# Routed experts: a third pair of buffers for the weighed outputs, the gather moved ahead of the scatter, and loads of weights released by the first half of a scatter

## The reference, cut to what matters

```python
x = x + 0.5 * ffn(layernorm(x)); x = x + attention(layernorm(x)); x = x + 0.5 * ffn(layernorm(x))
# ffn, h = the 4096 normalised tokens, xb[e] = the up to 192 tokens of expert e
g = einsum('ech,eih->eci', xb, w_gate); u = einsum('ech,eih->eci', xb, w_up)
yb = einsum('eci,ehi->ech', silu(g) * u, w_down)        # E = 32 experts, H = 512, I = 256
routed = sum over the 6 experts of a token of yb[expert, its slot] * its weight
return routed + shared_expert(h)
```

## Time and profile before

| | |
|---|---|
| median of 3 runs | 1670.54 us (1665.2 to 1672.09) |
| the profiled execution | 1662.59 us, span 1660.8 us |
| mean granted TensorE clock | 0.962 |
| busy in the span | PE 89%, DVE 66%, ACT 62%, POOL 45% |
| moved by DMA | 257.61 MB, mean 155 GB/s |

### The profile page before, as it was taken

How to read it: one execution, slowest core, us unless ns; L and a number is a source line. 1 busy time by engine, 2 the same in 40 slices (tenths; PEclk the granted TensorE clock), 3 DMA queues, 4 the chain that set the end, 5 groups by cost and what they waited for, 6 DMA issues and landing times. The chain is left out here.

```text
span 1660.8 us, 23985 instructions
## 1 busy us (share of the span) xinstructions
PE 1476.0 (89%) x8434; PEld 1226.3 (74%) x8436; DVE 1103.8 (66%) x2094; ACT 1028.3 (62%) x2046; POOL 754.6 (45%) x655
## 2 busy tenths in 40 slices
PE   5999969989894889999999999895999869998896
PEld 4877768877773678887887887774887758877775
DVE  5659848867672466766766765664649858776774
ACT  5861448777773476666666666654762528776774
POOL 0123225655554666565556655420113224665554
PEclk9999979999997799999999999997999979999998
DMA  7736388989895101111111111006654467998895
GB/s 275 246 126 207 99 260 249 266 257 265 258 264 87 52 26 46 39 58 52 39 39 64 39 39 39 30 35 232 204 178 153 144 205 231 259 270 250 263 257 104
DMA packets 113207, 257.61 MB, mean 155 GB/s; under 512 B 21216, under 2 KB 22176, under 8 KB 112832
## 3 DMA queue, kind: packets, MB, share of 16 engines
q1 hardware_dynamic: 90560, 204.16, 37.3%
q0 software_dynamic: 22528, 51.92, 13.8%
HBM read 187.27 MB, written 68.76 MB: 154 GB/s over the span
## 5 line engine op out<-in xcount | busy, mean ns | idle before, releaser
L989 DVE TENSOR_TENSOR e_w_lo<-e_raw,e_w_hi 128x1024 fp32r<-128x1024 f32 x192 | 233.9, 1219 | 31.2 <-ACT e_w_hi L925 29.6
L925 ACT ACTIVATE e_w_hi<-e_raw 128x1024 fp32r<-128x1024 f32 x192 | 202.3, 1054 | 20.8 <-PEq L273 20.8
L1490 POOL TENSOR_SCALAR t_prob<-t_prob,t_inv 128x128 f32<-128x128 f32 (+7 forms) x128 | 111.5, 871 | 221.3 <-DVE t_inv L1395 221.3
L901 POOL DMA_INDIRECT e_xg<-htab,slots x128 | 145.7, 1138 | 58.0 <-issue 38.4
L1063 PE MATMUL e_ps_gate<-e_xt,e_w_hi 128*128 128x384 f32 x512 | 159.3, 375 | 0.0
L909 POOL DMA_INDIRECT x_after_ffn<-e_y,slots x64 | 96.4, 1506 | 121.8 <-ACT e_y L954 83.9
L1063 PE MATMUL e_ps_up<-e_xt,e_w_hi 128*128 128x384 f32 x512 | 151.0, 360 | 0.0
L909 POOL DMA_INDIRECT out<-e_y,slots x64 | 95.7, 1495 | 120.9 <-ACT e_y L954 83.6
L357 POOL TENSOR_SCALAR d_inter<-d_inter 128x512 f32<-128x512 f32 x32 | 26.2, 818 | 266.9 <-DVE d_inter L521 266.8
L1290 ACT ACTIVATE t_prob<-a_wide,t_neg_max,a_q_scale 128x128 f32<-128x128 f32 (+7 forms) x128 | 106.5, 832 | 53.8 <-DVE t_neg_max L1389 53.5
L954 ACT ACTIVATE e_y<-e_ps_down,e_xg 96x512 f32<-96x512 f32 x128 | 83.1, 679 | 90.5 <-DMA out<-e_y,slots 34.2
(11 more groups left out here) (218 smaller groups left out, 4613.5 us busy)
## 6 DMA issues: line engine op xcount, KB each, us to landing
e_raw<-in_w_experts SPq DMA_DIRECT2D x192, 512.0 KB
htab<-d_h SPq DMA_DIRECT2D x16, 1024.0 KB, 5.2
d_x<-in_x SPq DMA_DIRECT2D x16, 512.0 KB, 6.9
d_xs<-in_x SPq DMA_DIRECT2D x32, 256.0 KB, 3.5
x_after_ffn<-d_xs SPq DMA_DIRECT2D x32, 256.0 KB, 3.2
q_x<-x_after_ffn SPq DMA_DIRECT2D x32, 256.0 KB, 3.0
t_res<-x_after_ffn SPq DMA_DIRECT2D x32, 256.0 KB, 2.6
x_after_attention<-t_res SPq DMA_DIRECT2D x32, 256.0 KB, 2.0
```

The source lines that it names most:

```text
L901: pool.indirect_dma_start(xg[e % GATHERED][q][:, :], None, htab, row).then_inc(gathered[e % GATHERED], 16)
L925: act.activation(third(w_hi[e % 2], c), third(raw[e % 3], c), ACT.Copy).then_inc(hi_ready, 1)
L989: dve.tensor_tensor(third(w_lo[e % 2], c), third(raw[e % 3], c), third(w_hi[e % 2], c).bitcast(F32), ALU.subtract).then_inc(lo_ready, 1)
L1490: pool.tensor_scalar(prob[:, u, 0:width(i)], prob[:, u, 0:width(i)], inv[:, u:u + 1], 1.0, ALU.mult, ALU.mult).then_inc(p_ready, 1)
```

## The change

1. `y` gets a third pair of buffers: `weigh(e)` waits for the scatter of e - 3 instead of e - 2, half by half. `silu`, `inter`, `in_hi` and `in_lo` go down to one buffer each.
2. `added` becomes two semaphores, one for each half. A scatter still waits for both halves of the one before. The load of the weights of e + 3 waits for the first half of the scatter of e - 3 alone.
3. GpSimd waits for `y_ready` of e, issues `gather(e + 5)`, and then waits for the landing of the scatter of e - 1 and issues `scatter(e)`.

```diff
-        silu = [sb(f"e_silu{u}_", [P, TC], F32) for u in range(2)]
+        silu = sb("e_silu", [P, TC], F32)
...
-        y = [[sb(f"e_y{u}{q}_", [HALF, D], F32) for q in range(2)] for u in range(2)]
+        y = [[sb(f"e_y{r}{q}_", [HALF, D], F32) for q in range(2)] for r in range(3)]
...
-        added = sem("e_added")
+        added = [sem(f"e_added{q}_") for q in range(2)]
...
                     if e >= 3:
-                        sp.wait_ge(added, 32 * (e - 2))
+                        sp.wait_ge(added[0], 16 * (e - 2))
...
                 def scatter(e):
-                    pool.wait_ge(y_ready, 2 * e + 2)
                     if e:
-                        pool.wait_ge(added, 32 * e)
+                        for q in range(2):
+                            pool.wait_ge(added[q], 16 * e)
...
-                        pool.indirect_dma_start(acc, row, y[e % 2][q][:, :], None, compute_op=ALU.add).then_inc(added, 16)
+                        pool.indirect_dma_start(acc, row, y[e % 3][q][:, :], None, compute_op=ALU.add).then_inc(added[q], 16)
...
                 for e in range(E):
-                    scatter(e)
+                    pool.wait_ge(y_ready, 2 * e + 2)
                     if e + GATHERED < E:
                         gather(e + GATHERED)
-                pool.wait_ge(added, 32 * E)
+                    scatter(e)
+                for q in range(2):
+                    pool.wait_ge(added[q], 16 * E)
...
                 def weigh(e):
-                    if e >= 2:
-                        act.wait_ge(added, 32 * (e - 1))
                     for q in range(2):
+                        if e >= 3:
+                            act.wait_ge(added[q], 16 * (e - 2))
                         act.wait_ge(d_ready, 2 * e + q + 1)
-                        act.activation(y[e % 2][q][:, :], ps_down[q][0:HALF, :], ACT.Copy,
+                        act.activation(y[e % 3][q][:, :], ps_down[q][0:HALF, :], ACT.Copy,
```

More of the change, by code:

```diff
@@ L836, in routed_experts @@
         gate_sum, up_sum = sb("e_gate_sum", [P, FB, CAP], F32), sb("e_up_sum", [P, FB, CAP], F32)
-        silu = [sb(f"e_silu{u}_", [P, TC], F32) for u in range(2)]
-        inter = [sb(f"e_inter{u}_", [P, TC], F32) for u in range(2)]
-        in_hi = [sb(f"e_in_hi{u}_", [P, TC], F32R) for u in range(2)]
-        in_lo = [sb(f"e_in_lo{u}_", [P, TC], F32R) for u in range(2)]
-        y = [[sb(f"e_y{u}{q}_", [HALF, D], F32) for q in range(2)] for u in range(2)]
+        silu = sb("e_silu", [P, TC], F32)
+        inter = sb("e_inter", [P, TC], F32)
+        in_hi = sb("e_in_hi", [P, TC], F32R)
+        in_lo = sb("e_in_lo", [P, TC], F32R)
+        y = [[sb(f"e_y{r}{q}_", [HALF, D], F32) for q in range(2)] for r in range(3)]
         ps_t = [pb(f"e_ps_t{i}_") for i in range(2)]
@@ L941, in gate @@
                     act.wait_ge(gate_sum_ready, e + 1)
-                    act.activation(silu[e % 2][:, :], gate_sum[:, :, :].rearrange("p b s -> p (b s)"),
+                    act.activation(silu[:, :], gate_sum[:, :, :].rearrange("p b s -> p (b s)"),
                                    ACT.Silu).then_inc(silu_ready, 1)
@@ L946, in split_inner @@
                     act.wait_ge(mul_ready, e + 1)
-                    act.activation(in_hi[e % 2][:, :], inter[e % 2][:, :], ACT.Copy).then_inc(ihi_ready, 1)
+                    act.activation(in_hi[:, :], inter[:, :], ACT.Copy).then_inc(ihi_ready, 1)
                 def weigh(e):
-                    if e >= 2:
-                        act.wait_ge(added, 32 * (e - 1))
                     for q in range(2):
+                        if e >= 3:
+                            act.wait_ge(added[q], 16 * (e - 2))
                         act.wait_ge(d_ready, 2 * e + q + 1)
-                        act.activation(y[e % 2][q][:, :], ps_down[q][0:HALF, :], ACT.Copy,
+                        act.activation(y[e % 3][q][:, :], ps_down[q][0:HALF, :], ACT.Copy,
                                        scale=xg[e % GATHERED][q][:, D + e:D + e + 1]).then_inc(y_ready, 1)
@@ L1008, in gate @@
                     dve.wait_ge(silu_ready, e + 1)
-                    dve.tensor_tensor(inter[e % 2][:, :], silu[e % 2][:, :], up_sum[:, :, :].rearrange("p b s -> p (b s)"),
+                    dve.tensor_tensor(inter[:, :], silu[:, :], up_sum[:, :, :].rearrange("p b s -> p (b s)"),
                                       ALU.mult).then_inc(mul_ready, 1)
@@ L1013, in split_inner @@
                     dve.wait_ge(ihi_ready, e + 1)
-                    dve.tensor_tensor(in_lo[e % 2][:, :], inter[e % 2][:, :], in_hi[e % 2][:, :].bitcast(F32),
+                    dve.tensor_tensor(in_lo[:, :], inter[:, :], in_hi[:, :].bitcast(F32),
                                       ALU.subtract).then_inc(ilo_ready, 1)
@@ L1086, in down @@
                             s = slice(b * CAP + q * HALF, b * CAP + (q + 1) * HALF)
-                            got = split_products(pe, ps_down[q][0:HALF, :], (in_hi[e % 2][:, s], in_lo[e % 2][:, s]),
+                            got = split_products(pe, ps_down[q][0:HALF, :], (in_hi[:, s], in_lo[:, s]),
                                                  (w[0][:, b, :], w[1][:, b, :]), b == 0, b == FB - 1)
```

## The result

The changed kernel takes 1657.68 us (median of 5 runs, 1650.48 to 1661.35), the kernel before, run beside it, 1670.54 us (median of 5); the ratio is 0.9938, 95% interval [0.9914, 0.9963]. So it is faster by 0.6%, some 10 us, where I had forecast 40. The execution that was profiled took 1661.35 us (span 1659.6 us), the slowest of the five, and the one of before 1662.59 us, so the two traces stand closer together than the medians do. What follows is read from rounds, not from the spans.

What follows compares the result with a forecast made beforehand. The loop from scatter to scatter was taken as the bound: 46.8 us gained by early release less 6.4 us for later starts gave 40.4 us less, a median of 1630 us; range of 8 in 10, 1612 to 1654.

Steps and rivals of the forecast that it cites:

- The bound: Middle rounds are paced scatter to scatter, 9.11 us each in the second call; weighing and y buffers are off that loop.
- The release: Weight loads start behind the scatter's first half, 0.9 us earlier against the landing of both: 46.8 us over 52 rounds.
- it follows at once and the round shrinks by 0.9 us: With weights ending 0.9 us earlier and descriptors ready by then, the scatter's data follow directly, shortening each round by 0.9 us.
- 1.8 us of scatter: Time in a round for the scatter's 0.39 MB to move once the weights are through.
- 1.5 us to the semaphore: Time in a round from the scatter's last byte until its landing is seen.
- L: The moment a scatter's landing is seen, from which times inside a round are counted.
- 4.8 us of weights: Time in a round for the weight load to move, ahead of the scatter's data.
- The scatter waits behind weights: A scatter issued after weights moves its data only once they are through; the forecast rests on this.
- The gather ahead: Gather issued before the scatter: nothing on the loop, but scatter 0 starts 3.2 us later per call, 6.4 us in all.
- The tail: Last rounds, scatter 27 to 31, without weights: 6.8 us each, expected to stay as they are.
- The second half: Rival: the scatter's second half is caught behind the early weights, slower, 1692 us; sign, landings over 12 us; chance 0.07.
- The queues share: Rival: scatter and weights share the DMA engines, so a scatter ends only 0.45 us sooner: 1653 us, chance 0.07.

Runs made afterwards that it cites:

- e1: The kernel before with only `added` split in two and weight loads released by the scatter's first half; two y buffers, gather behind scatter: ratio 0.9938.
- e3: The changed kernel with the scatter put in front of the gather again on POOL: ratio 0.9944.
- e14: The kernel before, second and third thirds of a weight load held until the next scatter is issued, first third released by the first half's landing: ratio 0.9715.
- e9: The changed kernel with the last two thirds of a weight load held until both halves of the next scatter are issued: ratio 0.9727.
- e6: The changed kernel with only the first half of an expert's tokens gathered from expert 5 on: ratio 0.9768.
- e10: The kernel before with only the first half of an expert's tokens gathered from expert 5 on: ratio 0.9953.
- e15: The changed kernel with the whole weight load held until the next scatter is issued, and no wait for a landing: 1613.85 us, ratio 0.9684.
- e13: The kernel before with the second and third thirds of a weight load held until the next scatter is issued: ratio 0.9800.
- e8: The changed kernel with the last third of a weight load held until both halves of the next scatter are issued: ratio 0.9827.
- e2: The changed kernel with weight loads waiting for both halves of the scatter again; third y buffer and gather ahead remain: ratio 1.0056.
- e12: The changed kernel with the last third of a weight load held until the first half of the next scatter is issued: ratio 0.9927.
- e4: The changed kernel with weight loads waiting for no scatter, without SyncE's wait for `added`: ratio 1.0016.

## Why the prediction was wrong

*The bound.* Right. The chain was scatter to scatter, and ScalarE's weighing only ran beside it. e1, which keeps two y buffers, is as fast as e3, which differs from it by the third pair (and the single buffers), and e14 is as fast as e9.

*The release.* Right as far as the first byte: loads 1.0 us ahead of the landing, and the scatter's data 0.81 us earlier on average. **The step that failed is the next one, "it follows at once and the round shrinks by 0.9 us".** It took the round for a sum of pieces one behind the other, held the last two, 1.8 us of scatter and 1.5 us to the semaphore, for fixed, and put the gathers outside. In its place the runs showed this. From its first data to its landing a scatter took 3.79 us instead of 3.23, so of 0.81 us gained 0.26 were left in the middle rounds (0.24 over 27 of them). And the gathers, free before, were part of the round: with half of them left out it fell to 8.29 us, the forecast's 8.2 nearly, while the same edit took 0.09 us off the kernel before (e6 and e10). How the gathers do it is shown in part. They move at the same time as the early weights and hold up the next scatter's data by 0.48 us (for half of them). Why the scatter's own stretch grew by 0.56 us stays open: leaving out half of the gathers shortens it by 0.2 us in both kernels, the scatter's packets took only 3% longer each, and POOL's slower issue was early enough.

*The 1.5 us to the semaphore* was misread in the earlier trace rows. Three packets of that scatter still start behind 1507.0, the last at L + 8.7, 0.6 us before the landing: most of the 1.5 us is the scatter's own late packets.

*What I could have read.* DMA was 0.89 busy before, in rounds of 9.11 us: 8.1 us of engine time. A round of 8.2 us asked for engines that are 0.99 busy and no slower for it. I named 1.8 us of scatter and 4.8 us of weights and never set the DMA share beside the new round. Yet the share is no hard floor either: e15 moves 301 GB/s at 1.04.

*The scatter waits behind weights.* Right in kind: e13, the kernel before with two thirds of the weights moved to the other side and nothing else of the change, is 2.0% faster, and e8, e9, e14 and e15 agree. But I used it for 0.9 us when it held the larger gain of 50 us.

*The gather ahead.* Its price at the start, 3.2 us, is in the trace of the second call to a tenth; in the time it shows in e2 and not in e3.

*The tail* stayed, as written: (1653.11 - 1625.82) / 4 = 6.8 us a round.

*The rivals.* The second half was not caught behind weights in the change (the longest round of either call took 10.4 us, where the sign was 12); e12 shows that it can be. "The queues share" had given 1653 us and came nearest, by luck: its sum rests on a scatter that shares with the weights from L + 2.8 on, and in 1526.5:1529.5 of the change no q0 packet moved. In e15 the two queues have 74.0% and 38.8% in the same half microsecond, but there it is gathers and weights that share. The Trainium skill's round-robin rule (DMA: Bandwidth & Descriptors, "Queues, rings and completion order") agrees with that row and not with 1503:1504 before, where q0 had no packet. For the scatter itself, the half microseconds of 1440:1580 in which its packets and the weights each had over 30% number 8 before, 13 in the change, and 35 and 39 in e4 and e12, where weights are issued without regard to it or between its halves. So it can share; what decides when it does was not tried.

## What to carry to other kernels

Where a chain of small dependent transfers shares the DMA engines with large loads, the order can decide, as it did here: try to issue the large load right behind a link of the chain, so that it moves during the link's completion and the next one's issue, and not right ahead of one. Before pricing an earlier start, multiply the DMA share by the round, and look up what now moves in the time that the start will take: that work is free only as long as the time is empty. Count a transfer's packets from the first to the landing, by size where two kinds share a queue, before holding that stretch for fixed. A buffer whose wait ends at the same landing as the chain's own is not in the chain, whatever name the profile gives to the wait.

## What was unexpected of the hardware

The DMA engines' busy share and their rate come apart: 0.95 busy gave 272 GB/s in the change, 0.96 gave 259 in e4, 1.04 gave 301 in e15, with the same packets in another order. A share of 1.04 over 90 us means that the recorded times of packets overlap on an engine, so the share does not say how much room is left.
